# Self-attention in a perceiver: maxima split in bf16 by GpSimd, turned and subtracted in single passes

## The reference

```python
x = x + L0_xattn(layernorm(x), ctx, mask, ...)   # 16 heads of 8, 2048 keys
x = x + L0_attn(layernorm(x), ...)               # causal self-attention, 128 keys
x = x + L0_ffn(layernorm(x), ...)                # one chosen 128x128 matrix
x = x + L1_xattn(layernorm(x), ctx, ...)
x = x + L1_attn(layernorm(x), ...)               # reversed mask, fill -10000
x = x + L1_ffn(layernorm(x), ...)                # router, 16 experts, 4 chosen
# self-attention, layer 1
scores = einsum('bhki,bhqi->bhkq', k, q) / sqrt(8)
scores = where(mask, scores, -10000.0)
probs  = softmax(scores, axis=2)
out    = einsum('bhkq,bhkl->bhql', probs, v)
```

## Time and profile before

| | us |
|---|---|
| median of three timed runs | 339.18 |
| lowest and highest | 338.36, 341.93 |
| the profiled execution | 338.62 |
| its span | 336.6 |
| TensorE busy | 288.2 (86%) |
| VectorE busy | 228.5 (68%) |
| ScalarE busy | 208.4 (62%) |
| GpSimd busy | 71.4 (21%) |

### The profile page before, as it was taken

How to read it: one execution, slowest core, us unless ns; L and a number is a source line. 1 busy time by engine, 2 the same in 40 slices (tenths; PEclk the granted TensorE clock), 3 DMA queues, 4 the chain that set the end, 5 groups by cost and what they waited for, 6 DMA issues and landing times.

```text
span 336.6 us, 10091 instructions
## 1 busy us (share of the span) xinstructions
PE 288.2 (86%) x4246; PEld 185.9 (55%) x4246; DVE 228.5 (68%) x374; ACT 208.4 (62%) x431; POOL 71.4 (21%) x136
## 2 busy tenths in 40 slices
PE   7808799999999997989548899999999993895786
PEld 5602467676667653744412576676767662443655
DVE  5926688878999944471546878878999913524572
ACT  5544588888988985115212788888898981152141
POOL 5500575000000015130000765000000000300033
PEclk9967799999999999589955999999999997899599
DMA  7944225522222803430000025321222000000000
GB/s 252 395 171 148 79 63 174 182 74 74 70 75 78 289 3 118 134 104 26 0 0 0 2 74 207 113 76 57 85 66 92 4 3 0 2 0 2 0 2 16
DMA packets 10688, 27.84 MB, mean 83 GB/s; under 512 B 2209, under 2 KB 3169, under 8 KB 10258
## 3 DMA queue, kind: packets, MB, share of 16 engines
q1 hardware_dynamic: 10568, 26.97, 24.0%
q10 hardware_dynamic: 74, 0.20, 0.2%
HBM read 20.74 MB, written 6.42 MB: 81 GB/s over the span
## 4 chain that ended last, share of the span: by engine, by line
PE 71%; DVE 10%; issue 8%; SPq 3%; DMA 3%; ACT 2%; POOL 2%; DVEq 0%; POOLq 0%
PE bank L923 69%; SPq L236 3%; DMA wB<-in_packB 2%; DMA k_scratch<-kparts 1%; DVE s_neg L760 1%; DVE kparts L663 1%; PE bank L957 1%; POOL y L324 1%; DVE k_rest L660 1%; DVE mx L692 1%; PE bank L1150 1%; ACT xnT L421 0%; DVE v_all L751 0%; PE bank L1186 0%; ACT mask_s L421 0%
## 5 line engine op out<-in xcount | busy, mean ns | idle before, releaser
L692 DVE TENSOR_REDUCE mx<-bank 128x2 f32<-128x1024 f32 x128 | 154.5, 1224 | 31.1 <-PE bank L923 28.9
L473 ACT ACTIVATE probs<-bank 128x512 f32<-128x512 f32 x256 | 139.3, 594 | 16.2 <-PE bank L923 10.8
L923 PE MATMUL bank<-q_exp,kpair 64*128 64x128 bf16 x1024 | 84.5, 218 | 2.1 <-DMA wB<-in_packB 1.5
L923 PE MATMUL bank<-kpair,q_rows 64*128 64x512 bf16 x256 | 75.1, 396 | 8.3 <-DMA kpair<-k_scratch 6.8
L923 PE MATMUL bank<-probs,v_all 128*9 128x128 f32 x2048 | 80.4, 275 | 1.1 <-ACT probs L473 1.0
L923 PEld LDWEIGHTS bank<-q_exp,kpair 64*128 64x128 bf16 x1024 | 55.5, 94 | 31.9 <-issue 17.8
L923 PEld LDWEIGHTS bank<-probs,v_all 128*9 128x9 f32 x2048 | 43.3, 90 | 15.7 <-ACT probs L473 4.0
L359 POOL CAST m_rows<-negm 128x2 bf16<-128x2 f32 x32 | 6.2, 193 | 162.7 <-DVE negm L699 162.7
L923 PEld LDWEIGHTS bank<-kpair,q_rows 64*128 64x128 bf16 x256 | 22.8, 94 | 17.2 <-issue 13.7
L421 ACT ACTIVATE v_all<-bank 128x256 f32<-128x256 f32 (+1 forms) x26 | 11.8, 454 | 10.4 <-PE bank L923 10.4
L324 POOL TENSOR_TENSOR y<-ve,mhalf 128x2 f32<-128x2 f32 x6 | 4.2, 697 | 52.5 <-DVE ve L642 52.5
(11 more groups left out here) (209 smaller groups left out, 351.4 us busy)
## 6 DMA issues: line engine op xcount, KB each, us to landing
k_scratch<-kparts SPq DMA_DIRECT2D x24, 256.0 KB, 2.7
kpair<-k_scratch SPq DMA_DIRECT2D x63, 96.0 KB
kpair<-k_scratch SPq DMA_DIRECT2D x63, 64.0 KB
ctxT_s<-in_ctxT SPq DMA_DIRECT2D x4, 512.0 KB, 5.9
mask_s<-in_mask SPq DMA_DIRECT2D x2, 1024.0 KB, 10.6
kpair<-k_scratch SPq DMA_DIRECT2D x63, 32.0 KB
wM<-in_packM SPq DMA_DIRECT2D x1, 1728.0 KB, 7.2
wB<-in_packB SPq DMA_DIRECT2D x1, 727.0 KB, 5.4
```

The source lines that it names most:

```text
L473: act.activation(probs[:, j % 4, :], bank[:, 4 + j % 2, :], ACT.Exp).then_inc(S("exp_done"), 1)
L692: V.tensor_reduce(mx[n % 2][:, w, :], bank[:, 2 * (w % 2):2 * (w % 2) + 2, :], AX.X, ALU.max) \
L923: return T.matmul(out_, lhsT=lhsT, rhs=rhs, start=start, stop=stop, **kw)
```

## The change

- VectorE writes the negated maxima densely (16 columns). GpSimd splits them in three bf16 parts (`s_parts`), which together hold the fp32 value: four dependent operations a batch, each behind a semaphore.
- TensorE first makes masks and scores of three banks, then turns the parts with four bf16 products by the identity into the fourth bank; a part stands in a row of its own, and the three parts of a head in the same 32 rows.
- The copy to `s_row` is bf16. The subtraction multiplies it by bf16 ones (`ones_b`), which adds up the three parts.
- For batch 0, VectorE copies the bank to `o_flat`, and `back(0)` moves ahead of the values of batch 1.
- The memset of `s_neg` becomes one of `s_parts`, and one of `ones_b` comes with it. The fp32 square of ones shrinks to a column.

```diff
-        s_neg = sb("s_neg", [P, B, 4 * (P + 1)])
-        s_row = wide[:, 6:8, :].rearrange("p b (j q) -> p b j q", j=4)
+        s_neg = sb("s_neg", [P, B, H])
+        s_rest = sb("s_rest", [P, B, H])
+        s_parts = sb("s_parts", [P, B, 4, P], BF16)
+        ones_b = sb("ones_b", [P, P], BF16)
+        s_row = wide[:, 6, :].bitcast(BF16).rearrange("p (b j q) -> p b j q", b=B, j=4)
...
+        def part_of(b, k):
+
+            return s_parts[:, b, :, :].rearrange("p j (g r) -> p g j r", r=32)[:, :, :, k]
...
+                for b in range(B):
+                    done = 4 * (2 * l + b)
+                    neg, rest = by_group(s_neg[:, b, :]), by_group(s_rest[:, b, :])
+                    pool.wait_ge(S("s_neg"), 2 * l + b + 1)
+                    pool.tensor_copy(part_of(b, 0), neg).then_inc(S("s_split"), 1)
+                    pool.wait_ge(S("s_split"), done + 1)
+                    pool.tensor_tensor(rest, neg, part_of(b, 0), ALU.subtract).then_inc(S("s_split"), 1)
+                    pool.wait_ge(S("s_split"), done + 2)
+                    pool.tensor_copy(part_of(b, 1), rest).then_inc(S("s_split"), 1)
+                    pool.wait_ge(S("s_split"), done + 3)
+                    pool.tensor_tensor(part_of(b, 2), rest, part_of(b, 1), ALU.subtract).then_inc(S("s_split"), 1)
...
-            pool.memset(s_neg[:, :, :], 0.0).then_inc(S("neg_zero"), 1)
+            pool.memset(s_parts[:, :, :, :], 0.0).then_inc(S("neg_zero"), 1)
+            pool.memset(ones_b[:, :], 1.0).then_inc(S("neg_zero"), 1)
+            pool.wait_ge(S("neg_zero"), 2)
...
-                for b in range(B):
-                    flat(b)
+                flat(1)
...
                 V.tensor_copy(s_row[:, 1, :, :].rearrange("p j q -> p (j q)"), bank[:, S_BANK[1][3], :]).then_inc(S("s_row"), 1)
+                dve.wait_ge(S("pv_self"), 8 * l + 4)
+                V.tensor_copy(o_flat[:, 0, :], bank[:, PV_BANK[0], :]).then_inc(S("o_flat"), 1)
...
-                    pe.wait_ge(S("s_neg"), 2 * l + b + 1)
+                    pe.wait_ge(S("s_split"), 4 * (2 * l + b + 1))
                     for j in range(4):
-                        last = T.transpose(bank[:, S_BANK[b][3], j * P:(j + 1) * P],
-                                           s_neg[:, b, j * P:(j + 1) * P], ident)
+                        last = mm(bank[:, S_BANK[b][3], j * P:(j + 1) * P], s_parts[:, b, j, :], ident_b[:, :])
...
-                        mm(bank[:, S_BANK[b][g], :], ones_sq[group(g), :],
+                        mm(bank[:, S_BANK[b][g], :], ones_b[group(g), :],
                            s_row[group(g), b, :, :].rearrange("p j q -> p (j q)"), start=False)                             .then_inc(S("st_done"), 1)
...
                 for b in range(B):
+                    pe.wait_ge(S("s_neg"), 2 * l + b + 1)
+                    turned(b, range(3))
                     neg_rows(b)
-                    turned(b)
+                    pe.wait_ge(S("s_row"), 2 * l + b + 1)
+                    turned(b, range(3, 4))
                     subtract(b)
                 for g in range(4):
                     values(0, g)
...
+                back(0)
                 for g in range(4):
                     values(1, g)
-                for b in range(B):
-                    back(b)
+                back(1)
```

More of the change, by code:

```diff
@@ L165, in perceiver_kernel @@
         flag_i = sb("flag_i", [1, 1], I32)
-        ones_sq = sb("ones_sq", [P, P])
-        ones_col = ones_sq[:, 0:1]
+        ones_col = sb("ones_col", [P, 1])[:, :]
         r_e = sb("r_e", [P, B, E])
@@ L213, in heads_ps, with by_group @@
             return bank[:, 7 - b, 256:256 + H * 9].rearrange("p (h c) -> p h c", c=9)
[L215 to L218 removed]
+        def part_of(b, k):
+            return s_parts[:, b, :, :].rearrange("p j (g r) -> p g j r", r=32)[:, :, :, k]
+        def by_group(v):
+            return v.rearrange("p (g j) -> p g j", g=4)
         def r_bank(k):
@@ L519, in exp_fill @@
                     act.wait_ge(S("s_neg"), 2 * l + b + 1)
-                    act.activation(e_fill[:, b, :].rearrange("p (g j) -> p g j", g=4),
-                                   s_max_of(b), ACT.Exp,
-                                   bias=B_("fill", 1)).then_inc(S("e_fill"), 1)
+                    act.activation(e_fill[:, b, :], s_neg[:, b, :], ACT.Exp, bias=B_("fill", 1)).then_inc(S("e_fill"), 1)
                 def exp_group(b, g):
@@ L615, in _ @@
                 V.memset(v_all[i][:, :, :, :, HD:VW], 1.0).then_inc(S("v_zero"), 1)
-            V.memset(ones_sq[:, :], 1.0)
+            V.memset(ones_col, 1.0)
             V.memset(r_gs[:, :, :], -BIG)
@@ L755, in s_max @@
                     dve.wait_ge(S("sa_done"), 2 * l + b + 1)
-                    neg = s_max_of(b)
-                    if l == 0 and b == 0:
-                        dve.wait_ge(S("neg_zero"), 1)
+                    neg = by_group(s_neg[:, b, :])
                     for i in range(2):
@@ L1146, in neg_rows, with turned @@
                 def neg_rows(b):
-                    pe.wait_ge(S("s_neg"), 2 * l + b + 1)
+                    pe.wait_ge(S("s_split"), 4 * (2 * l + b + 1))
                     for j in range(4):
-                        last = T.transpose(bank[:, S_BANK[b][3], j * P:(j + 1) * P],
-                                           s_neg[:, b, j * P:(j + 1) * P], ident)
+                        last = mm(bank[:, S_BANK[b][3], j * P:(j + 1) * P], s_parts[:, b, j, :], ident_b[:, :])
                     last.then_inc(S("neg_t"), 1)
-                def turned(b):
+                def turned(b, groups):
                     pe.wait_ge(S("k_s"), l + 1)
                     pe.wait_ge(S("qexp"), 2 * l + b + 1)
[L1158 to L1162, removed]
+                    mask(b, 1, groups)
+                    for g in groups:
                         mm(bank[:, S_BANK[b][g], :], k_s[group(g), b, :],
```

## The result

| | before | after |
|---|---|---|
| median, us (lowest to highest, executions) | 339.53 (338.36 to 341.93, 4) | 351.68 (348.6 to 353.9, 4) |
| profiled execution, us | 338.62 | 352.16 |
| its span, us | 336.6 | 350.0 |
| mean granted clock in the span | 0.919 | 0.878 |
| TensorE busy, us | 288.2 (86%) | 294.7 (84%) |

The changed kernel takes 1.0328 times as long, 95% interval 1.0241 to 1.0414. I had forecast 340.2, in a range up to 342.0. In all four executions the mean clock is low (0.864 to 0.882).

A forecast was written before the change was run, and what follows sets the result against it. Self-attention was taken as a single thread on TensorE, where every added wait is paid in full. Terms -0.16 - 0.16 + 1.58 + 0.31 = +1.57 on the profiled 338.62 gave 340.2 us, range 338.6 to 342.0.

The forecast's parts named there:

- the clock falls inside self-attention: Rival: in layer 0's tail TensorE drops to 1.2 GHz before the second value products, +2.7, 342.9 us; chance 0.10.
- Part 1: Self-attention's score blocks: 4.11 and 4.20 us, together 8.31 against 8.47, a gain of 0.16 us a layer.
- Part 2: Self-attention's tail, with batch 0's transposes ahead of batch 1's values: a loss of 1.58 us in layer 0, 0.31 in layer 1.
- The rule on GpSimd: Skill text: elementwise work belongs on VectorE, GpSimd takes about twice as long; set aside for rows of 0.19 to 0.20 us.
- the uncovered turn and copy: In each score block: turn and copy no longer hidden cost +0.55 to +0.65 us, about paid by the shorter subtraction's -0.64.

The follow-up runs named there:

- kernel with filled blocks: Changed kernel with three zero-weight products behind each turn in the blocks, none in the tail: median 342.04 us, before 338.85; ratio 1.0109.
- the order alone: Kernel before with only the new order of a block, all in fp32, old tail, nothing on GpSimd: median 345.85 us, before 339.06.
- the tail alone: Kernel before with only the change's tail, blocks and subtraction in fp32 and old order: median 342.44 us, before 339.06; ratio 1.0147.
- the interleaved kernel: Changed kernel with old tail, three banks and turn of both batches ahead of both last banks: 345.11, 346.65, 343.68 and 335.48 us, before 338.85.
- filled ahead: Changed kernel with four zero-weight products between the scores of batch 0 and batch 1, none in the blocks: median 346.77 us, before 337.77; ratio 1.015.
- the rounded one: Kernel before with maxima rounded to one bf16 number, bf16 turn and subtraction, old order and tail, no GpSimd: median 337.2 us, before 338.85; ratio 0.9971.
- the interleaved and filled one: Interleaved kernel with four zero-weight products ahead and two while TensorE waits for batch 1's maxima: median 338.62 us, before 337.77; ratio 1.0025.

## Why the prediction was wrong

**The failed step is the sum's silent assumption that the stage stays at full rate.** Every duration in it was a row at 2.4 GHz. The rival "the clock falls inside self-attention" named what happened, with the sign its own sentence gave it, but it had a chance of 0.10 and a price of 2.7.

- *Part 1, right at full rate.* With the waits filled the blocks take 154.91 - 150.82 = 4.09 and 159.10 - 154.91 = 4.19; forecast were 4.11 and 4.20. GpSimd's split was under cover as said: in the changed kernel its last operation ends 1.23 after the maxima, TensorE comes at 1.42. The turn took 0.43 until ScalarE's start, forecast 0.41 + 0.03; the bf16 subtraction took 0.30 until the next block (154.61 to 154.91), forecast 0.32.
- *Part 2, right at full rate.* The tail measures 164.08 - 159.10 = 4.98 there and 4.97 alone; forecast was 4.95. Layer 1's stage with filled waits is 13.33; forecast was 13.28. Structure together: +1.6 us, forecast +1.57. The kernel with filled blocks stands 3.2 us over its before (342.04 to 338.85); its mean clock is 0.008 lower, which at 1.7 to 2.2 us for 0.01 is 1.4 to 1.8, about the other 1.6 (a reckoning, not a measurement). So even with the rate restored the median lies at the top of my range.
- *The rule on GpSimd* would have made it 341.2. The rows decide: its four operations on 16 elements take 0.25, 0.23, 0.25 and 0.27, and 0.33 from start to start. I had compared GpSimd with VectorE's operations of other forms. The kernel before has the same chain of four on VectorE, on 32 elements, elsewhere in layer 1:

```profile
321.06 0.18 DVE L895 CAST comb_parts<-comb 128x32 bf16<-128x32 f32 x1
321.27 0.19 DVE L896 TENSOR_TENSOR comb_rest<-comb,comb_parts 128x32 f32<-128x32 f32 x1
```

  That is 0.18 and 0.19, and 0.21 to 0.23 from start to start. So GpSimd is slower by 20 to 40% for one operation and by half for the chain, at half the elements; the Trainium skill's factor of two for two inputs (GPSIMD Engine Reference, sections 3.1 and 4.1) is not reached at this size, but its direction is right and my "no more than VectorE's" was wrong. It cost nothing, because the chain lay under cover.
- *The clock rival, right in kind, wrong in place, number and price.* I let the clock fall once, late, in layer 0's tail. It fell in the first block of layer 0, 1.2 us after the copy gap ended, and at the same place in layer 1. I had looked for idle time in the tail, where the new wait is longest, and for the blocks I had only added up the gap of 0.69 as time. A row of the timeline before that I had not used could have warned that the stage isn't free of idle time, the one in front of the first block:

```profile
149.85 0.66 PE L1150 MATMUL bank<-wA,s_neg 128*128 128x128 f32 x4 [1.04 <-DVE s_neg L760]
```

  TensorE already stands still for 1.04 us there. The new gap begins 1.8 us after that one ends, in a stretch that was busy without a break before. That this nearness is what counts is not shown: with the old idle time filled the clock still fell in the second block. And the fall covers nearly all of the rest of the stage in the changed kernel: what has to be priced is the TensorE work behind it at nearly twice its length, 5.2 to 5.5 us a layer here. With the old tail it was half as long and cost 3.1.
- *The evidence.* Filling the gap with useless products restores the rate in the profile, lifts the mean clock of all 8 executions above that of the changed kernel, and takes 9.6 us off the median. Thin passes without a gap kept it in the profile, and their 10 executions are no slower than the kernel before. A thicker subtraction with the gap lost it in the profile (3 of 4 executions by time and mean clock). Undoing the tail shortens the falls but doesn't prevent them. Other idle time in the stage, the 2.32 us for the split, has the same effect.
- *Slips in the sums.* By its own terms the uncovered turn and copy cost +0.51 and +0.60, not +0.55 to +0.65, and the ends of the range come out at 338.7 and 341.8, not 338.6 and 342.0. Neither touches the forecast.
- *On transposes.* The prediction cited the Trainium skill (TensorE: Matmul & The Clock Gate, Part 4) for transposes not counting as work for the clock. No run here separates that from idle time: the tail, with four fp32 transposes between gaps of 0.8 and 0.7, kept its rate in the profiles in which it was reached at full rate.

What stays open: why one execution of the same program falls and the next does not (by their times the order alone splits 2 to 2, the tail alone 2 to 2, the interleaved kernel 3 to 1, filled ahead 2 to 2), where the clock fell in unprofiled executions, which are judged by their mean clock alone, and how much bf16 in place of fp32 adds to the likelihood of a fall; the order alone is long in half of its executions, the change in all four, which are too few to tell. In layer 0 of the interleaved kernel the clock fell before the second gap, 0.44 us long, was past, and why that stage falls and that of the kernel before does not is unexplained; it has 0.44 more idle time and cheaper products, and these two weren't separated there.

No version is measurably faster than the kernel before. The nearest are the rounded one (0.9971 [0.993, 1.0012]), which is not the same computation, and the interleaved and filled one (1.0025 [0.9987, 1.0064]).

## What to carry to other kernels

A wait that is put into a dense TensorE stretch has two prices: its own length, and the chance that the rest of the stage runs at half rate; here 0.7 us of wait brought 5 us. Idle time that already stands near it is a warning, though removing it didn't prevent the fall. Where a profile shows a granted clock of 0.50 that was 1.00 before the change, fill the wait with products by zeros, as an experiment, before anything else: if the clock and the time come back, the time was lost to the clock. And after shortening TensorE's passes, look who delivers the next operand: ScalarE's exponentials took back 0.5 of 1.8 us in one kernel and 0.85 of 1.13 in another.

## What the runs showed of the hardware

- Products with a weight matrix of zeros can keep the granted clock up: 1.00 in both stages in the profiles of the kernels with filled blocks, against 0.50 from 154.36 to 168.01 in the same program without them. Their place matters: four of them ahead of the maxima and none in the gaps did not (0.50 from 155.72).
- An added fall does not replace the next one. The kernel before falls at 169.93, during the following layer norms; the changed kernel had risen again at 168.01 and fell at 174.84 none the less. So here half rate in self-attention was paid on top.
- A stretch at half rate differs in length: 6.83 us in each stage with the old tail, 13.65 with the new one.
- The fp32 copy of 512 columns and the one that writes bf16 last the same on either engine: ScalarE 0.60, VectorE 0.69.
- At half rate the fp32 passes of six products took 2.08 against 1.13, the masks 0.64 against 0.42, and ScalarE's and VectorE's operations were unchanged (2.06 for four exponentials in both).
